# A fused linear-attention and gated-MLP kernel: projections ordered key, gate, value; first chunk products in float32; last norm tile by tile

## The chip, the cores and the metric

One core of a Trainium2 chip runs one program. The time is the device time of one execution in microseconds (us). Engines are named TensorE (PE in the profile), VectorE (DVE), ScalarE (ACT), GpSimd (POOL) and SyncE (SP, which here only issues DMAs).

## The reference

The input x is 8 sequences of 2048 tokens of 512 channels, in float32. Two layers follow each other:

```python
rkv = x @ W_rkv + b_rkv;  r, k, v = split(rkv);  r = sigmoid(r);  k = exp(k)
nu = exp(nu_log);  lam = exp(-nu);  gamma = exp(nu_log + gamma_log) - 1
u1[t] = lam * u1[t-1] + k[t] * v[t];   u2[t] = lam * u2[t-1] + k[t]
a = (u1 + gamma * k * v) / (u2 + gamma * k + 1e-6) * r
z = layernorm(x + a @ W_o + b_o)
xr, xk = mix of z[t] and z[t-1] by mu_r and mu_k
out = layernorm(z + sigmoid(xr @ W_r.T) * (relu(xk @ W_k.T)**2 @ W_v.T))
```

## The kernel before, in words

The 16384 tokens are 32 blocks of 512, 4 blocks to a sequence. The 512 channels are 4 chunks of 128 partitions. A block goes through two stages that are interleaved over two steps: in step s the three projections, the scans and the quotient of block s run, and between them the output product, the norm, the transposes and the second layer of block s-1. There are three program parts: `first_block`, `step` (written out for blocks 1 and 2, then in a loop over the sequences), and `finale`, which does the last block and all that is left. Each engine has its own order of calls, written out by hand, and waits on semaphores; nothing reorders it.

Products keep float32 accuracy by halves: every operand is split into a high part (float32r, a copy made by ScalarE) and a low part (value minus high, a subtraction by GpSimd or VectorE, written over the value). A product is then three matmuls: high by high, high by low, low by high. `project` (L1068) makes one projection of one chunk: 4 input chunks by 3 matmuls, 12 matmuls into one of four PSUM banks (bankA), used in turn; it waits until the bank's last user has read it. Of a chunk the order is key, value, gate. `rows_product` (L1097) does the same for the other four weights into bankB.

Per chunk VectorE runs `denominator` (L858: the scan of the key, the product of key and value, the denominator written into the key's buffer, the scaling by 1 + exp(-gate) and the reciprocal) and `numerator` (L884: the other scan and the sum). ScalarE runs `exp_key` (L595) and `exp_gate` (L604, two passes), GpSimd `att` (L410: numerator times reciprocal), ScalarE the high part `att_high` (L614), GpSimd the low part `att_low` (L415). `x_high` and `x_low` split the next block's input, which GpSimd does for block 1 (L408) and VectorE for the others; block 1's projections wait for them input chunk by input chunk.

At the start SyncE issues all loads, 12 of them before the rest of the projection weights. `write_columns` (L1091) is four dummy matmuls on the first weight that initialise bankB. The weights' low parts are made in block 0 and step 1 (`weight_A_low` for the projections, `weight_low` for the others). In the finale the last norm is made for two tiles of 128 tokens at a time (`inverse_std`, L419), with the last tile by itself (`last_factor`, `last_rows`).

## Time and profile before

| | us |
|---|---|
| median of 3 runs (2532.93 to 2536.94) | 2534.48 |
| the profiled execution | 2535.74 |
| its span, first to last instruction | 2533.9 |
| TensorE busy | 2510.5 (99%) |
| VectorE, ScalarE, POOL busy | 2013.6, 1267.5, 1245.6 |

The span is what the trace shows; the time of an execution has 1.84 us more around it. TensorE's busy time counts a matmul until its result is out, so that two that follow each other overlap: how far apart they start says what one costs.

### The profile page before, as it was taken

Reading aid. Unit: us, or ns where it says so; the run is one execution under the profiler, and the core shown is the slowest. Engines: PE = TensorE matmul, PEld = TensorE weight load, DVE = VectorE, ACT = ScalarE, POOL = GpSimd, SP = SyncE. Lnnn points to the kernel's source line nnn. Section 1 sums busy time; section 2 is a strip of 40 time slices with the busy share of each in tenths; the row PEclk is TensorE's granted clock in tenths of the full one; section 3 lists DMA queues with packets and bytes.
Section 4 is the critical chain, followed back from the end, with each engine's and each line's share of the span. In section 5 each row is a group of like instructions: output and inputs, shape, how many; then the busy total and the mean of one; then the engine's idle time right before and its main releaser. Section 6 shows DMA issues by size and latency. Waiting matters only on the chain.

```text
span 2533.9 us, 32904 instructions
## 1 busy us (share of the span) xinstructions
PE 2510.5 (99%) x11268; PEld 2076.7 (82%) x11268; DVE 2013.6 (79%) x2693; ACT 1267.5 (50%) x2157; POOL 1245.6 (49%) x1128
## 2 busy tenths in 40 slices
PE   7999999999999999999999999999999999999998
PEld 6888888888888888888888888888888888888877
DVE  7877888778787787887788777878777888787885
ACT  4545455444554444554545544455444555454545
POOL 6654454445454544535445444444444453545545
PEclk8999999999999999999999999999999999999999
DMA  4001110111100111111111011111111111110100
GB/s 170 26 34 51 45 39 34 34 51 50 34 34 34 51 51 34 46 38 35 51 39 45 34 35 50 50 34 34 35 50 50 34 43 34 43 51 34 51 25 34
DMA packets 57784, 110.63 MB, mean 44 GB/s; under 512 B 7040, under 2 KB 7040, under 8 KB 57088
## 3 DMA queue, kind: packets, MB, share of 16 engines
q1 hardware_dynamic: 57600, 108.31, 12.6%
q8 instruction: 100, 1.64, 0.3%
q14 instruction: 84, 0.69, 0.1%
HBM read 74.73 MB, written 33.55 MB: 43 GB/s over the span
## 4 chain that ended last, share of the span: by engine, by line
PE 98%; ACT 1%; POOL 0%; DVE 0%; DMA 0%; issue 0%; POOLq 0%; SPq 0%; DVEq 0%; ACTq 0%
PE bankA L1086 14%; PE bankA L1088 14%; PE bankA L1087 14%; PE bankB L1102 14%; PE bankB L1104 13%; PE bankB L1103 13%; PE bankB L1147 4%; PE bankB L1148 4%; PE bankB L1146 4%; PE bankB L1124 2%; PE bankA L1102 0%; PE bankA L1104 0%; PE bankA L1103 0%; POOL x_lo L408 0%; DMA wrkv_f<-in_w_rkv 0%; PE bankA L1148 0%
## 5 line engine op out<-in xcount | busy, mean ns | idle before, releaser
L1086 PE MATMUL bankA<-x_hi,wrkv_hi 128*128 128x512 f32 x1488 | 583.9, 392 | 4.7 <-POOL x_lo L408 4.7
L1088 PE MATMUL bankA<-x_hi,wrkv_lo 128*128 128x512 f32 x1488 | 580.5, 390 | 0.0
L1087 PE MATMUL bankA<-x_lo,wrkv_hi 128*128 128x512 f32 x1488 | 580.4, 390 | 0.0
L882 DVE RECIPROCAL gate<-gate 128x512 f32<-128x512 f32 x128 | 429.2, 3353 | 4.4
L413 POOL TENSOR_TENSOR att_f<-att_f,gate 128x512 f32<-128x512 f32 x128 | 209.4, 1636 | 280.1 <-DVE att_f L895 280.1
L1086 PEld LDWEIGHTS bankA<-x_hi,wrkv_hi 128*128 128x128 f32 x1488 | 280.3, 188 | 63.8 <-POOL x_lo L408 5.8
L1088 PEld LDWEIGHTS bankA<-x_hi,wrkv_lo 128*128 128x128 f32 x1488 | 280.1, 188 | 58.7
L1087 PEld LDWEIGHTS bankA<-x_lo,wrkv_hi 128*128 128x128 f32 x1488 | 280.4, 188 | 57.2
L424 POOL TENSOR_TENSOR ve<-mv,eps_ln 128x2 f32<-128x2 f32 x128 | 66.4, 519 | 462.6 <-DVE mv L907 459.6
L440 POOL TENSOR_TENSOR xk_lo<-xk_f,xk_hi 128x512 fp32r<-128x512 f32 x124 | 169.4, 1397 | 244.9 <-ACT xk_hi L667 244.9
L445 POOL TENSOR_TENSOR xr_lo<-xr_f,xr_hi 128x1024 fp32r<-128x1024 f32 x63 | 176.4, 2800 | 202.7 <-ACT xr_hi L672 202.7
L659 ACT ACTIVATE z<-z,shift,rstd 128x512 f32<-128x512 f32 x124 | 94.5, 809 | 297.6 <-POOL shift L433 297.6
L935 DVE SCALAR_TENSOR_TENSOR xr_f<-zT,vecs,xr_f 128x256 f32<-128x256 f32 x252 | 143.3, 628 | 123.7 <-ACT xr_f L644 123.7
L601 ACT ACTIVATE key<-bankA,b_sb 128x512 f32<-128x512 f32 x128 | 87.8, 686 | 283.9 <-PE bankA L1088 283.9
L879 DVE SCALAR_TENSOR_TENSOR gate<-key,gate 128x512 f32<-128x512 f32 x128 | 119.7, 935 | 125.4 <-ACT gate L612 123.2
L417 POOL TENSOR_TENSOR att_lo<-att_f,att_hi 128x512 fp32r<-128x512 f32 x128 | 186.8, 1460 | 32.8 <-ACT att_hi L616 32.8
L1102 PE MATMUL bankB<-wr_hi,xr_hi 128*128 128x512 f32 x504 | 199.5, 396 | 1.1 <-POOL xr_lo L445 1.1
L1103 PE MATMUL bankB<-wr_lo,xr_hi 128*128 128x512 f32 x504 | 196.4, 390 | 0.0
L1104 PE MATMUL bankB<-wr_hi,xr_lo 128*128 128x512 f32 x504 | 196.3, 389 | 0.0
L1102 PE MATMUL bankB<-wo_hi,att_hi 128*128 128x512 f32 x496 | 192.9, 389 | 0.0
L1103 PE MATMUL bankB<-wo_lo,att_hi 128*128 128x512 f32 x496 | 192.9, 389 | 0.0
L1104 PE MATMUL bankB<-wo_hi,att_lo 128*128 128x512 f32 x496 | 192.9, 389 | 0.0
(150 smaller groups left out, 5588.5 us busy)
## 6 DMA issues: line engine op xcount, KB each, us to landing
y<-in_x SPq DMA_DIRECT2D x128, 256.0 KB, 2.7
x_f<-in_xT SPq DMA_DIRECT2D x124, 256.0 KB, 4.0
out<-z SPq DMA_DIRECT2D x124, 256.0 KB, 2.1
wrkv_f<-in_w_rkv SPq DMA_DIRECT2D x3, 768.0 KB, 7.7
xk_f<-in_xT SPq DMA_DIRECT2D x4, 256.0 KB, 4.5
wo_f<-in_w_o SPq DMA_DIRECT2D x1, 1024.0 KB, 11.2
wk_f<-in_w_k SPq DMA_DIRECT2D x1, 1024.0 KB, 13.1
wr_f<-in_w_r SPq DMA_DIRECT2D x1, 1024.0 KB, 15.2
```

The lines of the kernel that those rows point to most:

```text
L413: pool.tensor_tensor(att_f[:, c], att_f[:, c], gate[:, c % 2], ALU.mult).then_inc(att_made, 1)
L417: pool.tensor_tensor(att_lo[:, c], att_f[:, c], att_hi[:, c], ALU.subtract).then_inc(att_lo_made, 1)
L440: pool.tensor_tensor(lo[:, c], value[:, c], hi[:, c], ALU.subtract).then_inc(xk_lo_made, 1)
L445: pool.tensor_tensor(lo[:], value[:], hi[:], ALU.subtract).then_inc(xr_lo_made, 1)
L882: dve.reciprocal(gate[:, c % 2], gate[:, c % 2]).then_inc(rec_made, 1)
L935: dve.scalar_tensor_tensor(out=value[:, c], in0=zT[:, c, HALF * half + 1:HALF * half + HALF + 1], scalar=vecs[:, 2, c:c + 1], in1=value[:, ...
L1086: pe.matmul(bank[:], w_hi, hi[:, h], start=(h == 0), stop=False)
L1087: pe.matmul(bank[:], w_hi, lo[:, h], start=False, stop=False)
L1088: last = pe.matmul(bank[:], w_lo, hi[:, h], start=False, stop=(h == NC - 1))
L1102: pe.matmul(bank[:], hi, w_hi[:, c], start=(c == 0 and not begun), stop=False, skip_group_check=begun)
L1103: pe.matmul(bank[:], hi, w_lo[:, c], start=False, stop=False, skip_group_check=begun)
L1104: last = pe.matmul(bank[:], lo, w_hi[:, c], start=False, stop=(c == NC - 1), skip_group_check=begun)
```

## The change

- The order within a chunk becomes key, gate, value (`ORDER`), with the weights' loads, high and low parts in that order too. `product` is a function of its own, called after `denominator` (in block 0 ahead of it for chunks 2 and 3). The denominator is written into the scan's buffer `u2` instead of the key's, so the key stays until the product has read it.
- In block 0 the projections of the last chunk (`EXACT`) are single float32 matmuls on the values, and so is the last chunk of block 0's output product. The low parts of these weights are made later, in step 1; block 0's input low part has a place of its own (`x_first_low`, in z's memory).
- The first weight and the five small vectors are issued by ScalarE's queue. SyncE's loads come in another order.
- `write_columns` is seven matmuls on a tile of zeros, which VectorE writes first.
- The last block's second norm is made tile by tile (`tile_gated`, `tile_statistics`, `tile_factors`, `tile_normalise`); the last tile's variance plus epsilon moves from GpSimd to VectorE. In the finale all engines have a changed order, in which also some work of the block before the last moves.

The core of the diff (indentation taken back; left out: names of semaphores, the same exchange of value and gate in bank waits, ScalarE's and VectorE's order in the finale, and `tile_gated`, `tile_statistics` and `tile_normalise`, which are the old functions for one tile):

```diff
+EXACT = (3,)
+WARM = 7
+KEY, VALUE, GATE = range(3)
+ORDER = (KEY, GATE, VALUE)
...
-return (xk_hi, xk_lo, xk_f) if s.first() else (x_hi, x_lo, x_f)
+return (xk_hi, x_first_low, xk_f) if s.first() else (x_hi, x_lo, x_f)
...
 def load_first(s):
     _, _, value = inputs(s)
     sp.dma_start(value[:, 0], xT[0, :, 0]).then_inc(x_first[0], 16)
-    load(w_A[0], wA_loaded[0])
     for c in range(1, NC):
         sp.dma_start(value[:, c], xT[0, :, c]).then_inc(x_first[c], 16)
     load(w_A[1], wA_loaded[1])
     load(w_A[2], wA_loaded[2])
-    sp.dma_start(b_sb[:], b_rkv).then_inc(s_small, 16)
-    for i, v in enumerate((nu_log, gamma_log, mu_r, mu_k)):
-        sp.dma_start(vecs[:, i], v).then_inc(s_small, 16)
     for i in range(3, len(w_A)):
         load(w_A[i], wA_loaded[i])
...
 def first_block(s):
     load_first(s)
+    load_weight(W_WO)
     load_xT(s.back(-1))
-    load_weight(W_WO)
+    load_weight(W_R)
+    load_weight(W_V)
     load_weight(W_K)
     load_rows(s, 0)
-    load_weight(W_R)
-    load_weight(W_V)
...
+def weight_A_low(c, place):
+    which = ORDER[place]
+    pool.wait_ge(wA_hi_made[place if c == 0 else 2 + c], 1)
+    if c in EXACT:
+        pool.wait_ge((k_ready, v_ready, r_ready)[which], c + 1)
     pool.tensor_tensor(wrkv_lo[:, c, which], wrkv_f[:, c, which], wrkv_hi[:, c, which], ALU.subtract)\
         .then_inc(wA_lo_made[c], 1)
...
+if i == W_WO and c == NC - 1:
+    pool.wait_ge(ready["WO"], NT)
 pool.tensor_tensor(lo[:, c], value[:, c], hi[:, c], ALU.subtract).then_inc(w_lo_made[i], 1)
...
+def tile_factors(s, tile):
+    one = slice(tile, tile + 1)
+    pool.wait_ge(ln_mean[1], s.count(NT, tile + 1))
+    pool.wait_ge(out_made, s.back(1).count(NT, tile + 1))
+    pool.tensor_tensor(ve[:, 1, one], mv[:, 1, one, 1], eps_ln[:, 0:1], ALU.add).then_inc(ln_var[1], 1)
+    pool.tensor_tensor(shift[:, 1, one], zero[:, 0:1, 0], mv[:, 1, one, 0], ALU.subtract)\
+        .then_inc(ln_negated[1], 1)
+    pool.wait_ge(ln_var[1], s.count(NH, tile + 1))
+    pool.tensor_tensor(rstd[:, 1, one], ve[:, 1, one], half_pow[:, 0:1], ALU.pow).then_inc(ln_rstd[1], 1)
+    pool.wait_ge(ln_negated[1], s.count(NH, tile + 1))
+    pool.wait_ge(ln_rstd[1], s.count(NH, tile + 1))
+    pool.tensor_tensor(shift[:, 1, one], shift[:, 1, one], rstd[:, 1, one], ALU.mult).then_inc(ln_shift[1], 1)
 def last_factor(s):
     tile = NT - 1
-    pool.wait_ge(last_mean, 1)
-    pool.tensor_tensor(ve[:, 1, tile:NT], mv[:, 1, tile:NT, 1], eps_ln[:, 0:1], ALU.add).then_inc(last_var, 1)
+    pool.wait_ge(out_made, s.back(1).count(NT, NT))
     pool.wait_ge(last_var, 1)
     pool.tensor_tensor(rstd[:, 1, tile:NT], ve[:, 1, tile:NT], half_pow[:, 0:1], ALU.pow)\
...
 def first_block(s):
     weight_A_low(1, 0)
     weight_A_low(1, 1)
-    weight_A_low(1, 2)
     weight_A_low(2, 0)
     weight_A_low(2, 1)
-    weight_A_low(2, 2)
+    weight_A_low(1, 2)
     att(s, 0)
     att_low(s, 0)
+    weight_A_low(2, 2)
     x_low(s.back(-1), 0)
-    weight_A_low(3, 0)
-    weight_A_low(3, 1)
+    x_low(s.back(-1), 1)
     att(s, 1)
+    x_low(s.back(-1), 2)
+    att_low(s, 1)
     weight_low(W_WO, 0)
-    x_low(s.back(-1), 1)
-    weight_A_low(3, 2)
+    att(s, 2)
+    x_low(s.back(-1), 3)
+    att_low(s, 2)
     weight_low(W_WO, 1)
-    att(s, 2)
-    att_low(s, 1)
-    x_low(s.back(-1), 2)
-    x_low(s.back(-1), 3)
+    att(s, 3)
     weight_low(W_WO, 2)
-    att(s, 3)
-    weight_low(W_WO, 3)
-    att_low(s, 2)
-    att_low(s, 3)
...
 if s1.first():
+    weight_low(W_R, 0)
     weight_low(W_K, 0)
+    weight_low(W_R, 1)
+    weight_A_low(3, 0)
+    weight_A_low(3, 1)
     weight_low(W_V, 0)
-    weight_low(W_R, 0)
-    weight_low(W_R, 1)
-    weight_low(W_R, 2)
-    weight_low(W_R, 3)
+    weight_low(W_V, 1)
     weight_low(W_K, 1)
+    weight_low(W_K, 2)
+    weight_low(W_K, 3)
 if s2.exists():
     residual(s2, 1)
     inverse_std(s2, 1, 1)
 inverse_std(s1, 0, 0)
 inverse_std(s1, 0, 1)
 if s1.first():
-    weight_low(W_K, 2)
-    weight_low(W_K, 3)
+    weight_low(W_R, 2)
+    weight_low(W_R, 3)
+    weight_low(W_V, 2)
+    weight_A_low(3, 2)
 att(s, 0)
-if s1.first():
-    weight_low(W_V, 1)
-    weight_low(W_V, 2)
...
+if s1.first():
+    weight_low(W_WO, 3)
...
 inverse_std(s1, 0, 1)
 att(s, 0)
 att_low(s, 0)
+mixed_keys_low(s1)
 att(s, 1)
-mixed_keys_low(s1)
+att(s, 2)
+mixed_gate_low(s1, 0)
 att_low(s, 1)
-att(s, 2)
 att_low(s, 2)
-mixed_gate_low(s1, 0)
 att(s, 3)
 att_low(s, 3)
...
+def load_constants():
+    _, _, value, source = w_A[0]
+    act.dma_start(value, source).then_inc(wA_loaded[0], 16)
+    act.dma_start(b_sb[:], b_rkv).then_inc(s_small, 16)
+    for i, v in enumerate((nu_log, gamma_log, mu_r, mu_k)):
+        act.dma_start(vecs[:, i], v).then_inc(s_small, 16)
...
-wait(act, scale_made, s.count(NC, c - 1))
+wait(act, den_made, s.count(NC, c - 1))
+wait(act, kv_made, s.count(NC, c - 1))
...
 def first_block(s):
+    load_constants()
+    weight_A_high(0)
     x_high(s, 0)
-    weight_A_high(0)
     x_high(s, 1)
     x_high(s, 2)
     x_high(s, 3)
     weight_A_high(1)
+    weight_A_high(2)
     decay()
     exp_key(s, 0)
     gamma_exp()
-    weight_A_high(2)
     weight_A_high(3)
     exp_gate(s, 0)
     weight_A_high(4)
     exp_key(s, 1)
     exp_gate(s, 1)
-    weight_A_high(5)
-    att_high(s, 0)
     x_high(s.back(-1), 0)
     x_high(s.back(-1), 1)
+    att_high(s, 0)
+    weight_high(W_WO)
+    weight_A_high(5)
     exp_key(s, 2)
+    att_high(s, 1)
     exp_gate(s, 2)
+    x_high(s.back(-1), 2)
+    weight_high(W_V)
+    weight_high(W_R)
     exp_key(s, 3)
-    weight_high(W_WO)
+    att_high(s, 2)
+    exp_gate(s, 3)
+    x_high(s.back(-1), 3)
+    att_high(s, 3)
     weight_high(W_K)
-    exp_gate(s, 3)
-    x_high(s.back(-1), 2)
-    x_high(s.back(-1), 3)
-    att_high(s, 1)
...
+    wait(dve, scale_made, s.count(NC, c))
     dve.tensor_tensor_scan(u2[:], lam_c, key[:, c % 2], state(s, 1, c), ALU.mult, ALU.add)\
         .then_inc(u2_scanned, 1)
-    dve.wait_ge(v_ready, s.count(NC, c + 1))
-    wait(dve, num_made, s.count(NC, c))
-    dve.scalar_tensor_tensor(out=kv[:], in0=bankA[(3 * c + 1) % NBANK][:], scalar=b_sb[:, 1, c:c + 1],
-                             in1=key[:, c % 2], op0=ALU.add, op1=ALU.mult).then_inc(kv_made, 1)
     dve.wait_ge(u2_scanned, s.count(NC, c + 1))
     dve.tensor_copy(carry[:, 1, c:c + 1], u2[:, TB - 1:TB]).then_inc(u2_saved, 1)
-    dve.wait_ge(kv_made, s.count(NC, c + 1))
-    dve.scalar_tensor_tensor(out=key[:, c % 2], in0=key[:, c % 2], scalar=gamma[:, c:c + 1], in1=u2[:],
+    dve.wait_ge(u2_saved, s.count(NC, c + 1))
+    dve.scalar_tensor_tensor(out=u2[:], in0=key[:, c % 2], scalar=gamma[:, c:c + 1], in1=u2[:],
                              op0=ALU.mult, op1=ALU.add).then_inc(den_made, 1)
     dve.wait_ge(den_made, s.count(NC, c + 1))
     dve.wait_ge(gate_plus1, s.count(NC, c + 1))
-    dve.scalar_tensor_tensor(out=gate[:, c % 2], in0=key[:, c % 2], scalar=EPS_DEN, in1=gate[:, c % 2],
+    dve.scalar_tensor_tensor(out=gate[:, c % 2], in0=u2[:], scalar=EPS_DEN, in1=gate[:, c % 2],
                              op0=ALU.add, op1=ALU.mult).then_inc(scale_made, 1)
     dve.wait_ge(scale_made, s.count(NC, c + 1))
     dve.reciprocal(gate[:, c % 2], gate[:, c % 2]).then_inc(rec_made, 1)
+def product(s, c):
+    dve.wait_ge(v_ready, s.count(NC, c + 1))
+    dve.wait_ge(key_exp, s.count(NC, c + 1))
+    wait(dve, num_made, s.count(NC, c))
+    dve.scalar_tensor_tensor(out=kv[:], in0=bankA[(3 * c + 2) % NBANK][:], scalar=b_sb[:, 1, c:c + 1],
+                             in1=key[:, c % 2], op0=ALU.add, op1=ALU.mult).then_inc(kv_made, 1)
...
 dve.wait_ge(last_mean, 1)
+dve.tensor_scalar(ve[:, 1, tile:NT], mv[:, 1, tile:NT, 1], EPS_LN, None, ALU.add).then_inc(last_var, 1)
...
 def first_block(s):
+    zero_operand()
     weight_A_low(0, 0)
     x_low(s, 0)
     x_low(s, 1)
     x_low(s, 2)
     x_low(s, 3)
     weight_A_low(0, 1)
+    weight_A_low(0, 2)
     constants()
-    weight_A_low(0, 2)
     gamma_minus1()
     denominator(s, 0)
+    product(s, 0)
     numerator(s, 0)
     denominator(s, 1)
+    product(s, 1)
     numerator(s, 1)
+    product(s, 2)
     denominator(s, 2)
     numerator(s, 2)
+    product(s, 3)
     denominator(s, 3)
     numerator(s, 3)
...
+tile_gated(s, 0)
+tile_gated(s, 1)
+tile_statistics(s, 0)
+tile_gated(s, 2)
+tile_statistics(s, 1)
+tile_statistics(s, 2)
 last_rows(s)
...
+if s.first() and c in EXACT:
+    pe.wait_ge(wA_loaded[place if c == 0 else 2 + c], 16)
+elif s.first() or s.second() and c in EXACT:
...
+if s.first() and c in EXACT:
+    last = pe.matmul(bank[:], w_f, value[:, h], start=(h == 0), stop=(h == NC - 1))
+else:
+    pe.matmul(bank[:], w_hi, hi[:, h], start=(h == 0), stop=False)
+    pe.matmul(bank[:], w_hi, lo[:, h], start=False, stop=False)
+    last = pe.matmul(bank[:], w_lo, hi[:, h], start=False, stop=(h == NC - 1))
...
 def write_columns():
-    pe.wait_ge(wA_hi_made[0], 1)
-    for bank in bankB:
-        pe.matmul(bank[:], wrkv_hi[:, 0, 0, 0], wrkv_hi[:, 0, 0], start=True, stop=True)\
+    pe.wait_ge(zeroed, 1)
+    for i in range(WARM):
+        pe.matmul(bankB[i % NBANK][:], x_hi[:, 0, 0:P], x_hi[:, 0], start=True, stop=True)\
             .then_inc(columns_written, 1)
...
+if name == "WO" and s.first() and c == NC - 1:
+    pe.wait_ge(att_made, NC)
+    last = pe.matmul(bank[:], att_f[:, c, tokens_at:tokens_at + P], wo_f[:, c], start=False, stop=True,
+                     skip_group_check=begun)
+    break
...
 pe.wait_ge(sum_begun, s.count(NT, tile + 1))
-if tile == 0:
-    pe.wait_ge(att_lo_made, s.count(NC, NC))
 if s.first():
+    pe.wait_ge(att_first_lo, NC - 1)
+    pe.wait_ge(w_lo_made[W_WO], NC - 1)
+elif tile == 0:
+    pe.wait_ge(att_lo_made, s.count(NC, 0))
+if s.second():
     pe.wait_ge(w_lo_made[W_WO], NC)
```

In the finale ScalarE's order changes so that `att_high(s, 3)` comes ahead of `key_square(s1, 2)` instead of behind it, and `normalise_result(s1, 0)` ahead of `tanh(s, 0)`. In a middle step VectorE calls `product(s, c)` right behind `denominator(s, c)`; there are no other changes of order in it.

## Rows read from the trace of the kernel before

**Rows 1.** The page: the span, and the chain that ended last, by engine.
```profile
span 2533.9 us, 32904 instructions
...
PE 98%; ACT 1%; POOL 0%; DVE 0%; DMA 0%; issue 0%; POOLq 0%; SPq 0%; DVEq 0%; ACTq 0%
```

**Rows 2.** TensorE's waits from 0 to 130 us: total, times, longest us.
```profile
PE bankA L1086 <- POOL x_lo L408: 4.7, 2, 4.1
PE bankA L1086 <- POOL wrkv_lo L397: 4.0, 1, 4.0
```

**Rows 3.** TensorE's waits from 2380 us to the end.
```profile
PE bankB L1102 <- POOL xr_lo L445: 1.1, 1, 1.1
PE bankA L1102 <- POOL att_lo L417: 0.8, 1, 0.8
```

**Rows 4.** The chain, its longest pieces: start, us, what.
```profile
57.13 0.80 PE bankA L1086
88.05 1.75 PE bankB L1124 x16
...
2353.13 1.75 PE bankB L1124 x16
```

**Rows 5.** Stretches: us; busy PE, PEld, DVE, ACT, POOL; granted clock; DMA share, GB/s.
```profile
43.90:49.20 5.30, 5.30 (x13) 4.14 (x14) 5.23 (x7) 0.00 (x0) 4.14 (x2) 0.50 0.00 0
54.90:62.80 7.90, 7.32 (x16) 5.29 (x17) 7.02 (x7) 2.33 (x2) 7.90 (x5) 0.50 0.19 53
80.00:2440.00 2360.00, 2359.94 (x10643) 1954.61 (x10642) 1895.59 (x2542) 1184.26 (x2031) 1142.89 (x1032) 1.00 0.12 41
```

**Rows 6.** TensorE's timeline at the start: start, us, line, operation.
```profile
6.04 2.07 PE L1094 MATMUL bankB<-wrkv_hi 128*128 128x512 f32 x4 [6.04 <-ACT wrkv_hi L575]
7.91 0.63 PE L1086 MATMUL bankA<-xk_hi,wrkv_hi 128*128 128x512 f32 x1
...
11.75 0.43 PE L1086 MATMUL bankA<-xk_hi,wrkv_hi 128*128 128x512 f32 x1
```

**Rows 7.** ScalarE and SyncE's queue at the start.
```profile
0.74 1.28 ACT L570 ACT_TABLE_LOAD   x1 [0.74 <-PEq L1266]
...
1.19 0.43 SPq L307 DMA_DIRECT2D wrkv_f<-in_w_rkv  x1
...
5.36 0.63 ACT L575 ACTIVATE wrkv_hi<-wrkv_f 128x512 fp32r<-128x512 f32 x1 [0.21 <-DMA wrkv_f<-in_w_rkv]
```

**Rows 8.** VectorE in block 0: two scans and a scaling.
```profile
26.70 1.22 DVE L864 TENSOR_TENSOR_SCAN u<-lam,key 128x512 f32<-128x512 f32 x1
...
36.60 1.21 DVE L864 TENSOR_TENSOR_SCAN u<-lam,key 128x512 f32<-128x512 f32 x1
...
39.49 0.69 DVE L879 SCALAR_TENSOR_TENSOR gate<-key,gate 128x512 f32<-128x512 f32 x1
```

**Rows 9.** POOL and ScalarE late in block 0.
```profile
46.53 2.14 POOL L413 TENSOR_TENSOR att_f<-att_f,gate 128x512 f32<-128x512 f32 x1 [0.62 <-DVE att_f L895]
...
49.39 0.69 ACT L609 ACTIVATE gate<-bankA,neg_br 128x512 f32<-128x512 f32 x1 [7.92 <-PE bankA L1088]
...
50.65 1.13 ACT L570 ACTIVATE x_hi<-x_f 128x512 fp32r<-128x512 f32 x2
...
53.60 3.47 POOL L408 TENSOR_TENSOR x_lo<-x_f,x_hi 128x512 fp32r<-128x512 f32 x2
```

**Rows 10.** POOL in the last stage.
```profile
2460.85 1.68 POOL L413 TENSOR_TENSOR att_f<-att_f,gate 128x512 f32<-128x512 f32 x1 [2.14 <-DVE att_f L895]
2463.93 1.27 POOL L417 TENSOR_TENSOR att_lo<-att_f,att_hi 128x512 fp32r<-128x512 f32 x1 [1.39 <-ACT att_hi L616]
```

**Rows 11.** POOL's first instruction for the last tile.
```profile
2529.91 0.19 POOL L450 TENSOR_TENSOR ve<-mv,eps_ln 128x1 f32<-128x1 f32 x1
```

**Rows 12.** POOL and TensorE in a middle block.
```profile
1187.04 5.46 POOL L440 TENSOR_TENSOR xk_lo<-xk_f,xk_hi 128x512 fp32r<-128x512 f32 x4 [8.13 <-ACT xk_hi L667]
...
1191.22 0.39 PE L1146 MATMUL bankB<-xk_hi,wk_hi 128*128 128x512 f32 x1
```

More of the change, by code:

```diff
@@ L57, in first, with second @@
         return self.batch is None and self.s == 0
+    def second(self):
+        return self.batch is None and self.s == 1
     def last(self):
@@ L329, in store @@
                 for tile in range(HT * half, HT * half + HT):
-                    if tile in usual(s, half):
+                    if not s.last() or tile < NT - 1:
                         sp.wait_ge(out_made, s.count(NT, tile + 1))
@@ L898, in statistics @@
             def statistics(s, which, half, rows, made):
-                tiles = usual(s, half) if which else range(HT * half, HT * half + HT)
+                tiles = range(HT * half, HT * half + HT)
                 for tile in tiles:
```

179 lines of the change are left out of this document (101 added, 78 removed).

## Prediction

> **What bounds the kernel now.** I read first the page and the chain of waits, then TensorE's own waits stretch by stretch, then each engine's timeline in the first 80 us, in one middle block and in the last 80 us. The span is 2533.9 us and the chain runs 98% over TensorE [rows 1]. Between 80 and 2440 us TensorE is busy 2359.94 of 2360 us [rows 5]; its waits all lie at the two ends: 4.0 us and twice (4.7 us together, the longest 4.1) in the first 130 us [rows 2], and 1.1 and 0.8 us in the last stage [rows 3]. A middle block takes (2353.13 - 88.05) / 29 = 78.11 us; less 1.75 us of transposes it is 336 matmuls of 0.227 us [rows 4], so a group of 12 takes 2.73 us. A change that leaves the matmuls of a middle block alone can only win at the ends. There the prize is TensorE's late start, at 7.91 us with its first projection [rows 6], its pauses, and the half clock after them: the granted clock is 0.50 from 43.9 to 49.2 us and from 54.9 to 62.8 us, after pauses of 4.0 and 4.1 us [rows 2, 5]. A matmul at that level takes (11.75 - 7.91) / 9 = 0.427 us [rows 6], 0.200 more than at the full one.
>
> The point that fixes all the rest is 57.13 us [rows 4]: there the last quarter of block 1's input low part is done, TensorE has 9 matmuls of block 1 behind it, and from there it runs on without a pause to the last stage.
>
> **The start, after the change.** ScalarE issues the first weight load and five vectors itself: six issues of about 0.43 us, the price of the same issue on SyncE's queue, from 0.74 to 3.3 us, then its table load of 1.28, so 4.6 us [rows 7]. The weight lands 4.2 us after its issue if the times now (issued 1.19, its copy started 5.36, [rows 7]) hold, at 4.9. ScalarE's copy 0.63 [rows 7], VectorE's two subtractions of about 0.6 each: the first projection starts at 6.9 instead of 7.91. The four dummy matmuls that held TensorE until then become seven on a zeroed tile; they need no load, and seven of 0.427 end near 4.3, before the data, so they cost nothing. If the table load were placed ahead of the issues, the weight would land 1.3 us later and the gain would be gone. What they do to the clock is a rival below. In the forecast the clock rises as before, 5.7 us after TensorE starts in earnest (6.04 to 11.75, [rows 6]), at 12.6. By then 13.4 matmuls are done; group 2, now the gate's, ends at 12.6 + 10.6 x 0.227 = 15.0, and the third chunk's value, group 9, at 15.0 + 7 x 2.73 = 34.1.
>
> **The first block's chain.** VectorE's chain, not TensorE, decides when block 1 can start. One chunk cycles in 36.60 - 26.70 = 9.9 us; from its scan to its scaling 39.49 - 36.60 = 2.9, from the scaling to the end of the numerator the other 7.0 [rows 8]. With the gate second, chunk 0's scaling can start at 15.1 + 1.3 (gate's two passes, 50.65 - 49.39, [rows 9]) = 16.4. Then 7.0 and the product, a pass like the scaling, 0.7 [rows 8], now behind the reciprocal: next scan at 24.1, against 26.70 now. Chunk 1 ends at 34.0. Chunk 2's product waits until 34.3, 0.3 us. POOL's att takes 2.1 [rows 9] to 36.1, ScalarE's copy 0.6 to 36.7, and only behind this copy comes gate 2, to 38.0; scale, reciprocal and numerator 7.0, to 45.0. Then in ScalarE's and POOL's new order: att 2.1 (47.1), its copy 0.6 (47.7), gate 3 1.3 (49.0), the last input copy 0.6 (49.6), and POOL's subtraction, 1.27 to 1.74 ([rows 10]; 3.47 / 2, [rows 9]): **51.2 us, against 57.13: 5.9 earlier.** The order before had both last subtractions behind a gate that waited for TensorE until 49.39 [rows 9].
>
> **Float32 products.** Twelve matmuls replace 36 in block 0's last chunk and 4 replace 12 in its output product. No row shows one of 512 columns. Below it is bounded by the float32 transposes, 1.75 / 16 = 0.109 per 128 columns, 0.44 per 512 [rows 4]; above, the three products that it replaces take 0.68, and a full product of both operands' halves has a fourth, 0.91. I take 0.91, the row of a matmul of this shape being nearer than a transpose. The Trainium skill ("FP8 and Floating Point Precision") counts "True FP32: 4 passes through PE array"; by that too it is 0.91, and by the transposes' row 0.44. In the projections 12 x 0.91 = 10.9 instead of 8.2 lies under the chain above: TensorE ends block 0 at 34.1 + 10.9 = 45.0, does 9 matmuls of block 1 by 47.0 and waits until 51.2. The cover gone, it would be +2.7. In the output product nothing covers it: 4 x 0.23 = **+0.9** (from -1.0 to +0.9). That pause is 4.2 us, like the two that dropped the clock, so the half clock after it is paid again as before: no term.
>
> **Behind it.** From 51.2, TensorE has 39 matmuls, near 11.5 us with the half clock, before the output product at 62.7. That needs att 3 and three parts of the output weight: POOL has them at about 60 (numerator 3 ends 7.0 after gate 3, at 56.0; att 2.1, one subtraction of 1.7, [rows 9]), 2.7 ahead. Then POOL has ten weight subtractions, 13 to 17 us, before the norm's factors, so to 77 at the latest. The transposes are due at 62.7 + 11.8 + 8.2 = 82.7, and the 5.7 us between hold eight short POOL instructions and four ScalarE passes, half of them side by side, some 4 us by like passes [rows 9, 11]. Slack 1.7. Loads come in another order, but the one that ScalarE reads first, the output weight, is moved ahead.
>
> **Middle blocks.** The matmuls are the same. The product moves behind the reciprocal, which delays the key mix by 0.5 to 0.7 us in VectorE's queue; behind it wait ScalarE's high and POOL's low parts and TensorE's keys. The last low part is made at 1187.04 + 5.46 = 1192.50, and needed at 1191.22 + 9 x 0.227 = 1193.26 [rows 12]: 0.76 of slack, above both. Bank waits change names (value for gate): a bank is asked for three groups later, 8.2 us, and the product is at most 7.0 behind [rows 8]. The denominator in the scan's buffer needs a wait between two VectorE instructions, under 0.1 us and hidden by the same slack. Zero.
>
> **Last stage.** POOL's new order puts the gate's low part ahead of one att_low (1.3 us or more, [rows 10]), so its 1.1 us wait goes [rows 3]; the next wait then ends on chunk 3's att_low, whose att is done at 2462.5 and its low part at 2465.2 [rows 10]. With its copy one key square earlier this is 0.7 sooner: **-0.7** for both waits together. Per-tile norm: the last tile's own chain stays; only one POOL instruction (from 2529.91, [rows 11]) goes to VectorE: **-0.1**, 0 to -0.3.
>
> **Sum.** -5.9 + 0.9 - 0.7 - 0.1 = -5.8. The profiled execution took 2535.74, 1.84 around its span, and gives 2529.9; it lies 1.26 above the median of three, 2534.48, on which basis I forecast **2528.7**.
>
> **The rivals.**
> - *The dummies release the clock.* TensorE works from about 1.3 to 4.3, pauses 2.6 us, and is at full clock for the first projection. For: pauses of 1.1 us and less kept it [rows 3]. Against: 3 us of work is less than any stretch after which a row shows it rise, 5.7, 5.3 and 7.9 us [rows 5, 6]. It would save up to 11 matmuls of 0.2, and the whole chain moves with them: -2.2, so 2526.5. The Trainium skill ("TensorE: Matmul & The Clock Gate", Part 1) says that "activity releases the throttle"; that alone does not tell these two apart, and the rows decide the chance: 0.2.
> - *The clock survives the pause in block 1.* A float32 matmul of 1.1 us or a chain that is 1.5 us faster makes the pause some 2.5 us, and the half clock goes: -2.7 (13 x 0.2), so 2526. Rows show only that 4 us lose it. 0.08.
> - *The chain is later.* POOL's subtractions at 1.74 each and slow numerators beside them put block 1's input at 53 to 54, or the table load comes first: gain 2 to 4.5, so 2530 to 2532.5. 0.22.
> - *Slower: the key mix is late in each middle block.* If the shift is over 0.76, TensorE waits in all 30 blocks; at 0.95 the waits, 30 x 0.19, cancel the gain, and at 1.2 they are 30 x 0.44 = 13 us, which ends near 2542. Against: ScalarE is busy with its previous-keys pass in that time, so the mix is not what it waits for. 0.07.
> - *The ends cancel*, as a new wait of 3 to 6 us for the output weight or the norm: 2532 to 2537. 0.05.
>
> **The numbers.** Forecast 0.38, from 2527 to 2530.5. A measurement of this kernel tells about 0.2%, 5.1 us, from no change. Faster than 2529.4: most of the forecast case, its half below 2528.7 surely, and both clock rivals: 0.57. Same: the rest of it, the late chain and the cancelled ends: 0.36. Slower: 0.07. The range runs from both clock rivals together, 2523.8, to the late end of the third, 2533.5.
>
> **What would show it.** 11239 matmuls; TensorE busy without a break from 80 to 2430 us and blocks of 78.1; float32 matmuls near 0.9; the first projection at 6.9; block 1's last input part at 51.2 with the clock at 0.50 behind it; output product without a wait near 62.7; one wait of about 1.6 in the last stage. A middle block over 78.2, or a first input part later than 53, makes the prediction wrong.

## The result, and the profile after

The changed kernel takes **2543.34 us** (median of 7 runs, 2542.72 to 2545.03) against 2534.48 (7 runs, 2532.93 to 2536.94): a ratio of 1.0035, 95% interval [1.0026, 1.0044]. It is slower, by 8.9 us; the forecast was 2528.7, in a range from 2523.8 to 2533.5. The profiled execution took 2542.95 with a span of 2541.2, 7.3 more than before [rows 1].

The page of the changed kernel: span; the chain by engine; the queue that brings instructions (packets, MB, share of 16 engines).
```profile
span 2541.2 us, 32904 instructions
...
PE 94%; issue 2%; POOL 2%; DVE 1%; ACT 0%; DMA 0%; POOLq 0%; DVEq 0%
...
q8 instruction: 106, 1.74, 0.3%
```
Against [rows 1], "issue" is new with 2% of the chain: time in which an engine waited for nothing that the profile shows. Only part of the 2% are the pauses that follow: a_pad6 below, which has none of them, still has 1% of "issue" in its chain. TensorE's waits (us in total, times, longest) answer to [rows 2, 3]. The first four rows are of 0 to 130 us, the fifth of 130 to 2380 us, where the kernel before had none at all, the last two of the last stage.
```profile
PE bankA L1172 <- POOL x_lo L417: 3.5, 1, 3.5
PE bankA L1172 <- DVE x_first_low L886: 3.1, 1, 3.1
PE bankB L1180 <- DVE x_hi L890: 1.5, 1, 1.5
PE bankB L1240 <- POOL xk_lo L449: 0.6, 2, 0.3
...
PE bankA L1173 <- issue: 14.5, 6, 2.8
...
PE bankB L1240 <- POOL xk_lo L449: 1.2, 1, 1.2
PE bankB L1193 <- ACT xk_f L740: 0.7, 1, 0.7
```
The fifth row is the result in one line: six times in the steady state TensorE stands up to 2.8 us at the second matmul of a block, though nothing is late. Six is the number of times that its loop over batches jumps back. The chain shows the same in its transposes, one group a block (start, us, what).
```profile
160.54 1.75 PE bankB L1218 x16
...
472.28 1.75 PE bankB L1218 x16
553.39 1.75 PE bankB L1218 x16
...
787.21 1.75 PE bankB L1218 x16
869.24 1.75 PE bankB L1218 x16
...
2360.40 1.75 PE bankB L1218 x16
```
The block from 472.28 to 553.39 takes 81.11 us and that from 787.21 to 869.24, four blocks later, 82.03. A block in which the loop doesn't jump takes 77.9. So the time can be split at two rows: the transposes of the second block that pass, and those 28 blocks later.

| us of the span | before | after |
|---|---|---|
| to the second block's transposes | 166.16 | 160.54 |
| 28 blocks from there | 2186.97 | 2199.86 |
| the rest | 180.77 | 180.80 |

The start gained 5.6, the end nothing, and the middle, which the prediction put at zero, lost 12.9. The next question was what the loop's jump costs in one kernel and not in the other.

TensorE's timeline of the changed kernel at the first of the six places (start, us, line, operation, idle before it):
```profile
519.91 0.39 PE L1195 MATMUL bankB<-wv_hi,xk_lo 128*128 128x512 f32 x1
520.17 0.49 PE L1172 MATMUL bankA<-x_hi,wrkv_hi 128*128 128x512 f32 x1
523.48 0.39 PE L1173 MATMUL bankA<-x_lo,wrkv_hi 128*128 128x512 f32 x1 [2.82 <-issue]
```
The block's first matmul runs and its second, which needs nothing new, comes 3.31 us later. The packets of the instruction queue carry 1.64 MB / 100 = 16.4 KB each (1.74 / 106 after). The Trainium skill ("Runtime: NRT & Kernel Launch", "Instruction fetch mechanics") tells of refills "in **16 KiB blocks** (256 instructions)" and of a fetch that a taken branch must wait for; the packets agree with the size.
### The profile page after: what moved, and what is told of

Its sections match the earlier page's. It is cut to its first block, busy times and chain, and to the rows that moved or that the text cites. A ratio compares the mean times of both kernels' runs of the same rounds, so it can differ in the third digit from the quotient of the medians.

```text
span 2541.2 us, 32904 instructions
## 1 busy us (share of the span) xinstructions
PE 2509.6 (99%) x11255; PEld 2075.1 (82%) x11255; DVE 2099.5 (83%) x2693; ACT 1270.9 (50%) x2157; POOL 1252.2 (49%) x1130
## 3 DMA queue, kind: packets, MB, share of 16 engines
q8 instruction: 106, 1.74, 0.3%
## 4 chain that ended last, share of the span: by engine, by line
PE 94%; issue 2%; POOL 2%; DVE 1%; ACT 0%; DMA 0%; POOLq 0%; DVEq 0%
PE bankB L1193 13%; PE bankB L1194 13%; PE bankB L1195 13%; PE bankA L1173 13%; PE bankA L1172 13%; PE bankA L1174 13%; PE bankB L1240 4%; PE bankB L1242 4%; PE bankB L1241 4%; PE bankB L1218 2%; POOL xk_lo L449 0%; DVE att_f L939 0%; POOL wk_lo L412 0%; DMA wrkv_f<-in_w_rkv 0%; POOL att_f L422 0%
## 5 line engine op out<-in xcount | busy, mean ns | idle before, releaser
L1173 PE MATMUL bankA<-x_lo,wrkv_hi 128*128 128x512 f32 x1488 | 580.3, 390 | 14.5 <-issue 14.5
L449 POOL TENSOR_TENSOR xk_lo<-xk_f,xk_hi 128x512 fp32r<-128x512 f32 x124 | 178.8, 1477 | 241.2 <-ACT xk_hi L707 241.2
L920 DVE SCALAR_TENSOR_TENSOR gate<-u,gate 128x512 f32<-128x512 f32 x128 | 182.9, 1429 | 104.2 <-ACT gate L647 101.8
L984 DVE SCALAR_TENSOR_TENSOR xr_f<-zT,vecs,xr_f 128x256 f32<-128x256 f32 x252 | 150.0, 655 | 113.3 <-ACT xr_f L679 113.3
L478 POOL TENSOR_TENSOR z<-t,z 128x512 f32<-128x512 f32 x124 | 169.0, 1383 | 103.2 <-DVE t L1029 103.2
L426 POOL TENSOR_TENSOR att_lo<-att_f,att_hi 128x512 fp32r<-128x512 f32 x127 | 199.1, 1568 | 35.4 <-ACT att_hi L651 35.4
L1240 PE MATMUL bankB<-xk_hi,wk_hi 128*128 128x512 f32 x496 | 193.4, 390 | 1.9 <-POOL xk_lo L449 1.7
L1242 PE MATMUL bankB<-xk_hi,wk_lo 128*128 128x512 f32 x496 | 193.0, 389 | 0.0
## 6 DMA issues: line engine op xcount, KB each, us to landing
wo_f<-in_w_o SPq DMA_DIRECT2D x1, 1024.0 KB, 12.4
```

The costliest lines, as they stand in the source:

```text
L426: pool.tensor_tensor(att_lo[:, c], att_f[:, c], att_hi[:, c], ALU.subtract)\
L920: dve.scalar_tensor_tensor(out=gate[:, c % 2], in0=u2[:], scalar=EPS_DEN, in1=gate[:, c % 2], op0=ALU.add, op1=ALU.mult).then_inc(scale_ma ...
L1173: pe.matmul(bank[:], w_hi, lo[:, h], start=False, stop=False)
L1240: pe.matmul(bank[:], wk_hi[:, c, cols], hi[:, c], start=(c == 0), stop=False)
L1242: last = pe.matmul(bank[:], wk_lo[:, c, cols], hi[:, c], start=False, stop=(c == NC - 1))
```

## The experiments

All padding is of waits on a semaphore that has long reached its value; 12 of them make 6 more instructions on the page, 474 make 237. "Left" is the number of instructions from the loop's head to the end of its piece of 256.

**a_pad6 and a_warm4: the loop's head of the changed kernel moved.** By six instructions later (place 1 of the next piece, 255 left) and six earlier (place 245, 11 left):
```
 def write_columns():
     pe.wait_ge(zeroed, 1)
+    for _ in range(12):
+        pe.wait_ge(zeroed, 1)
```
```
-WARM = 7
+WARM = 4
```

> The changed kernel with twelve waits on an already reached semaphore behind the first one of TensorE, which come to six more instructions ahead of its loop; nothing else. Theory J (the place of the loop's head in TensorE's instruction stream, which the change moved by 19 instructions, makes every jump back wait for a second instruction fetch): the six pauses of 2.0 to 2.8 us marked issue behind the jumps vanish, the time is 2543.3 less about 16 us, so 2526 to 2529, and the instruction packets of q8 fall from 106 to about 100. Rival W (a wait that the new order of work brings once in a sequence of four blocks): nothing moves, 2542 to 2545.

> The changed kernel with four dummy matmuls instead of seven, which takes six instructions away ahead of the loop. Theory J: by my count 11 instead of 5 instructions are then left in the fetched piece behind the jump, six more that TensorE can do before it waits, so each pause is shorter by 3 x 0.227 = 0.7 us and the six by 4.1: 2539, near. Rival W: 2543. Theory C (the seven dummies shorten the half clock at the start): it would be up to 2 us longer than the changed kernel from the start alone, seen in the first 20 us and not at the jumps.

**b_pad237 and b_pad243: the same with the kernel before.** 237 more instructions, laid into the projections of blocks 1 and 2, bring its head to 251 of 256; 243 bring it to place 1:
```
+spare = [474]          # 486 in b_pad243
 def project(s, c, which):
     ...
+        if s.batch is None and 1 <= s.s <= 2:
+            for _ in range(min(6, spare[0])):
+                pe.wait_ge(columns_written, NBANK)
+                spare[0] -= 1
```

> The kernel before with 474 waits on an already reached semaphore among the projections of blocks 1 and 2, which come to 237 more instructions of TensorE ahead of its loop and put the loop's head where I count it in the changed kernel, 5 instructions before the end of a piece of 256. Theory J: the kernel before gets the same six pauses of 2 to 3 us, and its time goes from 2534.5 to about 2551; q8 has about 106 packets. Rival W: it has none of the new order, so no pause, 2534.5 plus what 237 waits cost themselves.

> The same with six more instructions, 243, which put the loop's head behind the end of the piece. Theory J: no pauses, 2534.5 plus what the waits themselves cost (near nothing, since TensorE's sequencer runs ahead), and 16 us less than with 237. Rival W, or waits that cost by their number: the same as with 237 or slightly more.

**b_n30 and b_n20: how many instructions must be left.** The same edit with 424 and 444 waits.

> The kernel before with 424 satisfied waits (212 more instructions in TensorE's stream) ahead of its loop, so that 30 of the 256 instructions of the fetched piece are left from the loop's head on. The runs of the changed kernel give, with 5 left, a largest gap of matmul starts after a jump of 2.4 to 3.3 us, and, with 11 left, pauses that sum to 8.9 us over six jumps. Theory of the fetch: after a jump the next piece comes about 3.2 us after the first, and each instruction that is left buys the length of one (312.5 us for the loop's 2800 or so, 0.11 us each), so 30 hide all of it: no pause after the jumps, 2534.5 us (2532.5 to 2536.5), as with 242 left. Rival, that any second fetch close behind the jump costs its full 2.8 us: 2551 us, six pauses.

> As before, with 444 satisfied waits (222 more instructions): 20 left. Theory of the fetch: 3.2 less 20 times 0.11, about 1.0 us after each of six jumps, so about 6 us: 2540.5 us (2536 to 2544), and the largest gap after a jump near 1 us. Rival with the full price: 2551 us; if the price ends earlier than that sum says, 2534.5 us and no pause.

Measured, with the sum of TensorE's waits for "issue" between 130 and 2380 us, and the 28 blocks from the second block's transposes on:

| kernel | left | time, us | ratio to before | issue, us | 28 blocks, us |
|---|---|---|---|---|---|
| before | 242 | 2534.48 | | 0 | 2186.97 |
| b_pad243 | 255 | 2534.51 | 0.9998 [0.9989, 1.0007] | 0 | 2186.83 |
| b_n30 | 30 | 2538.34 | 1.0014 [1.0005, 1.0023] | 0.2 | 2189.41 |
| b_n20 | 20 | 2542.63 | 1.0032 [1.0020, 1.0044] | 7.4 | 2195.52 |
| b_pad237 | 5 | 2559.89 | 1.0099 [1.0083, 1.0114] | 16.8 | 2212.61 |
| a_pad6 | 255 | **2524.66** | 0.9958 [0.9945, 0.9972] | 0 | 2182.60 |
| a_warm4 | 11 | 2537.36 | 1.0008 [0.9999, 1.0017] | 8.9 | 2193.18 |
| after | 5 | 2543.34 | 1.0035 [1.0026, 1.0044] | 14.5 | 2199.86 |

The place of the loop's head decides, in both kernels and in both directions. Twelve waits that do nothing take 18.7 us off the changed kernel, and six instructions fewer of padding cost the kernel before 25 us. The three dummies that a_warm4 lacks change nothing at the start: its second block's transposes come at 160.45 us, in the changed kernel at 160.54. This doesn't hang on the fitted 95: six instructions more end the pauses in both kernels, so the head lay within the last six places of its piece. The loop has 2883 records in every version, so its end moves with its head, and no run moved one alone; but the pauses end where the head crosses into the next piece, and grow as fewer instructions are left behind it. The fetches agree: behind the first jump the third piece is asked for 4.7 us after the second in the changed kernel (536.36 after 531.70), and 23.4 us after it in a_pad6 (554.94 after 531.52).

That more instructions cost time by themselves is out: the 243 of b_pad243 cost nothing. The full price for every second fetch is out too: with 20 left the pause is 1.4 us at the longest, with 30 one of 0.2 us is left. My sum of 0.11 us for each instruction left was a little high: from 5 to 20 the longest pause of the kernel before falls from 2.8 to 1.4 us, 0.09 an instruction, so b_n20 came at 2542.6 where 2540.5 was expected, still in its bounds; b_n30's 2538.3 is above its bounds by 1.8. Its trace has 2.6 us more in the 28 blocks than b_pad243's (0.43 a jump), with six waits of TensorE's weight loads for "issue", 2.8 us together; but the profiled execution was its fastest, 2535.74, and what the median has above that stands in no trace. In the changed kernel 11 left already bring the pause down from 2.8 to 1.6, a steeper fall, and what sets the difference stays open.

b_pad237 lost more than its pauses: 2212.61 - 2186.83 = 25.8 us against 16.8. Its granted clock shows five stretches of 3.4 us at half behind five of the six pauses; 5 x 1.7 = 8.5 makes up the rest. The changed kernel has one such stretch in the loop: 14.5 + 1.7 = 16.2 of its 2199.86 - 2182.60 = 17.3 us.

**a_order: the projections of a chunk back in the order key, value, gate.** The changed kernel with the padding of a_pad6, and the product back between scan and denominator.
```
-ORDER = (KEY, GATE, VALUE)
+ORDER = (KEY, VALUE, GATE)
 ...
 def denominator(s, c):
     ...
+    product(s, c)
     dve.wait_ge(u2_scanned, s.count(NC, c + 1))
```
Bank indices and bank waits follow the order, and the separate calls of product go.

> The changed kernel with its loop's head moved out of the bad place (12 waits on a satisfied semaphore ahead, as in the run that took 2524.7 us), and the projections of a chunk back in the order key, value, gate, with the product of value and key back between the scan of the denominator and its end. Theory, by the rows of the two traces: what the middle of the kernel gained (a period of 77.94 in place of 78.10 us, some 28 times, with TensorE's wait for the low part of the mixed receptance input) came from the order, so the period goes back to 78.1 and the time up by about 4 us; ahead of block 1 the values wait a chunk longer for nothing, up to 3 us more: 2530 us (2527.5 to 2532.5). Rival, the gain of the middle came from something else (the denominator in the scan's buffer, which took a wait away): the period stays at 77.94 and the time within 1.5 us of 2524.7 apart from the first block's part.

It took 2538.11 us (2537.17 to 2539.16), ratio 1.0011 [1.0002, 1.0020], 13.4 more than a_pad6 and 5.6 above the upper bound that was expected. The rows of its chain that answer to those of a_pad6:
```profile
163.93 1.75 PE bankB L1209 x16
...
2352.86 1.75 PE bankB L1209 x16
```
```profile
160.66 1.75 PE bankB L1220 x16
...
2343.26 1.75 PE bankB L1220 x16
```
The 28 blocks take 2188.93 us in a_order and 2182.60 in a_pad6: 78.18 and 77.95 a block; before, 78.11. The start is 3.3 later and the end, 182.74 in place of 180.74, 2.0, which was not expected at all. So the gain of the middle did come from the order, of the projections and of the product's place together (no run parts the two), and it was worth 6.3, not 4. What it took away shows in the waits of TensorE's weight loads between 130 and 2380 us (us in total, times, longest), first the kernel before, then a_order, then a_pad6:
```profile
PEld bankB L1102 <- POOL xr_lo L445: 5.2, 20, 0.3
PEld bankB L1102 <- issue: 2.2, 8, 0.3
```
```profile
PEld bankB L1184 <- POOL xr_lo L454: 6.6, 20, 0.3
PEld bankB L1184 <- issue: 2.7, 8, 0.4
```
```profile
PEld bankA L1172 <- issue: 0.4, 2, 0.2
```
Twenty times in 28 blocks a weight load of the gate's product came up to 0.3 us late, behind the low part of its input. With the gate computed second that wait is gone, and with it some 9 us of late loads, of which 6.3 were time. A reading of the queues suggests why (ScalarE makes this input's high part behind the gates' exponentials, which now come sooner), but no run took that apart. For the prediction I had read only the matmuls' rows of the waits and "busy 2359.94 of 2360" [rows 5]; a late weight load makes no pause there and shows in the loads' own rows alone.

**a_keys: in the last stage, the low part of the mixed keys ahead of attention's.**
```
     att(s, 0)
+    mixed_keys_low(s1)
     att_low(s, 0)
-    mixed_keys_low(s1)
     att(s, 1)
```

> The changed kernel with its loop's head moved (as in the run of 2524.7 us), and in the last stage GpSimd makes the low part of the mixed keys of the last block but one ahead of the low part of attention's first chunk of the last block. Theory: the order that the change gave there makes TensorE wait 1.2 us for this low part, which goes; the wait for its float part on ScalarE (0.7 us) stays: about 1.2 us less from the last loop's end to the end, 2523.5 us. Rival: attention's low part is then late and takes the wait over, nothing changes or up to 1 us more: 2524.7 to 2525.7 us. The stage in the trace decides, since the total can't tell 1 us surely.

2529.11 us (2527.6 to 2530.36), ratio 0.9974 [0.9965, 0.9983]: 4.5 more than a_pad6. The theory fell. TensorE's waits in the last stage of a_keys:
```profile
PE bankA L1195 <- POOL att_lo L426: 4.1, 1, 4.1
PE bankB L1195 <- ACT xk_f L740: 0.7, 1, 0.7
```
The 1.2 us wait is gone, and one of 4.1 for attention's last low part stands behind it, with 3.4 us of half clock after it. From the last loop's transposes (2341.45 in its timeline) to the end it takes 184.9 us, in a_pad6 (2343.09) 180.9. The rival had the mechanism right and the price, up to 1 us, far too low. So in the last stage two low parts wait for the same engine, and to put one first is paid by the other.

**a_xhigh: the last part of block 1's input first on ScalarE.**
```
     exp_key(s, 3)
+    x_high(s.back(-1), 3)
     att_high(s, 2)
     exp_gate(s, 3)
-    x_high(s.back(-1), 3)
```

> The changed kernel with its loop's head moved (as in the run of 2524.7 us), and ScalarE makes the high part of block 1's last input chunk right behind the last exponential of the key of block 0, ahead of attention's high part 2 and the last gate. In the trace of the changed kernel this chunk's low part ends at 50.84 us and TensorE stands 3.5 us, then runs at the lower clock for some 2.8 us. Theory: the chunk is ready about 2.5 us earlier, the pause falls to about 1 us, and the half clock behind it goes too, since it comes of the pause: about 4 us less, 2520.7 us. Rival: the pause shrinks by 2.5 us and the clock falls all the same, or the later attention parts (high part 2, the last gate) hold block 0's output product up by as much: 2522.2 us, or 2524.7 us with a new wait of TensorE for attention's last low part.

2525.79 us (2524.29 to 2526.0), ratio 0.9965 [0.9951, 0.9978]; a_pad6 has 0.9958. TensorE's waits in its first 120 us, without the two for the dummies and the first projection:
```profile
PE bankB L1195 <- POOL wo_lo L412: 2.1, 1, 2.1
PE bankA L1172 <- POOL x_lo L417: 1.7, 1, 1.7
PE bankB L1242 <- POOL xk_lo L449: 1.2, 3, 0.6
PE bankB L1220 <- ACT z L688: 1.0, 1, 1.0
```
The pause fell from 3.5 to 1.7 us, and the half clock behind it is gone, as the theory had it: in this trace the granted clock stays full from there to the end of the matmuls. But 2.1, 1.0 and 1.2 us of new waits in block 1 take it all back, as the rival's second half had it, if under other names. The cause of the first stands in the two engines' timelines, GpSimd and VectorE of a_xhigh:
```profile
45.96 2.19 POOL L417 TENSOR_TENSOR x_lo<-x_f,x_hi 128x512 fp32r<-128x512 f32 x1
48.11 1.74 POOL L426 TENSOR_TENSOR att_lo<-att_f,att_hi 128x512 fp32r<-128x512 f32 x1
49.80 1.73 POOL L412 TENSOR_TENSOR wo_lo<-wo_f,wo_hi 128x512 fp32r<-128x512 f32 x1
...
47.31 1.38 DVE L916 SCALAR_TENSOR_TENSOR u<-key,gamma,u 128x512 f32<-128x512 f32 x1
48.73 1.66 DVE L920 SCALAR_TENSOR_TENSOR gate<-u,gate 128x512 f32<-128x512 f32 x1
```
GpSimd's subtractions now run beside VectorE's two passes of two inputs, and both pay: 2.19 in place of 1.40 us, and 1.38 and 1.66 in place of 0.75 and 0.69 in a_pad6. VectorE, whose last scan starts 1.0 us earlier than in a_pad6, starts the reciprocal behind it 0.6 later (50.43 against 49.85), and the third low part of the output weight ends 0.4 later (59.26 against 58.91) for a TensorE that asks for it some 4 us sooner. The Trainium skill ("SBUF — State Buffer", "SBUF: two separate sides") says that the two engines share a pair of ports, which one of them holds for a whole instruction; the longer times of these rows agree, though they don't show how long either holds it.

**a_xhigh_wo: the third low part of the output weight in GpSimd's idle time.**
```
     att_low(s, 2)
     weight_low(W_WO, 1)
+    weight_low(W_WO, 2)
     att(s, 3)
-    weight_low(W_WO, 2)
```

> The changed kernel with its loop's head moved and the last input chunk's high part earlier, and GpSimd makes the third low part of the output weight ahead of attention's last chunk in block 0, not behind it. In the run without this second move the half clock was gone, but TensorE stood 2.1 us for this low part, which ended at 59.3 us, while GpSimd stood idle for 4.4 us ahead of attention's last chunk. Theory: the low part is made in that idle time, the wait goes, and the gain of the earlier input chunk comes to the end: 2523.5 us (2521.5 to 2525), and TensorE's block 1 starts some 2 us earlier. Rival: the low part then runs beside VectorE's reciprocal and scan, delays the last numerator and with it attention's last chunk; the wait changes its name only: 2525.5 us or more.

2524.73 us (2524.36 to 2525.11), ratio 0.9962 [0.9948, 0.9975]. That lies within the theory's bounds, but the gain didn't come. The wait for the weight went, but its name only changed: TensorE now waits 2.0 us for ScalarE's z, the norm's result, and behind that pause it runs at the half clock for 3.4 us, which a_xhigh did not have. The 16 transposes behind the wait take 2.71 us in place of 1.75:
```profile
79.36 2.71 PE bankB L1220 x16
```
The waits for the mixed keys in block 1 are gone in this trace. So the next chain in block 1, the norm, is as late as the one removed.

**a_sploads: the first weight and the vectors back on SyncE's queue.**
```
 sp.dma_start(value[:, 0], xT[0, :, 0]).then_inc(x_first[0], 16)
+load(w_A[0], wA_loaded[0])
```
and the vectors' loads behind the third piece of the weight; load_constants goes.

> The changed kernel with its loop's head moved (as in the run of 2524.7 us), and the first weight and the vectors back on SyncE's queue. Theory: the move saved nothing, since the weight landed 5.0 us after its issue from ScalarE in place of 4.2 us from SyncE behind the first input part; the first projection starts at 7.9 us as in both traces, and the total stays within 0.5 us of 2524.7 us. Rival, as the prediction had it: the move was worth 1.0 us and the later issue of the first input chunks costs more, the first projection starts at 8.9 us or so, 2525.7 us.

2525.08 us (2524.73 to 2525.4), ratio 0.9963 [0.9950, 0.9977]. The move is worth nothing in the total. The first projection starts at 7.56 us, in the six traces with the loads on ScalarE and the same padding at 7.77 to 8.06: if anything, SyncE's queue is the earlier. The weight is issued at 1.19 us and lands 4.25 later, at 5.44; in the changed kernel at 0.75, and lands 5.02 later, at 5.77.

**a_best: a_keys and a_xhigh together.**

> The changed kernel with its loop's head moved, the last input chunk's high part earlier, and in the last stage the mixed keys' low part ahead of attention's. Theory: the two parts lie 2,400 us apart and add: 4 and 1.2 us less than 2524.7, 2519.5 us (2517.5 to 2522), faster than both kernels (the kernel before 2535, the changed one 2543.3). Rival, if each of the two is worth nothing by itself: 2524.7 us.

2529.60 us (2528.42 to 2531.92), ratio 0.9981 [0.9972, 0.9990]: 10 above what was expected, and as a_keys alone, since a_xhigh is worth nothing. The best version stays a_pad6, 2524.66 us, with a_xhigh_wo level: 0.42% faster than the kernel before and 0.73% than the changed one.

## Why the prediction was wrong

**The step that failed.** "Middle blocks. The matmuls are the same. [...] Zero", with "TensorE busy without a break from 80 to 2430 us". I followed the data through the middle and not the instructions. Six jumps of the loop cost 17.3 us there (2199.86 - 2182.60, after against a_pad6), because the change made TensorE's stream ahead of the loop 19 instructions shorter and put the loop's head 5 instructions ahead of the end of its piece. Against this the 28 blocks gained 2186.97 - 2182.60 = 4.4 us by the new order, which was put at zero too. Neither was among the rivals, though the prediction's own sign of being wrong, a middle block over 78.2, came true in six blocks. The rival that ended slower, near 2542, has about the right time for a wrong reason: the last low part of the mixed keys did slip, but only from 0.76 to 0.4 us ahead (made at 1188.90 + 5.83 = 1194.73, needed at 1193.10 + 9 x 0.227 = 1195.14), and no middle block waits for it.

**What the other steps gave.** Without the jumps the sum of the change is -5.6 at the start, -4.4 in the middle and 0.0 at the end, -10.0, and a_pad6 measured 2524.66 - 2534.48 = -9.8. The prediction had -5.8.

- *The start*: 6.9 predicted, 7.89 measured, so nothing gained on 7.91. The term that was mis-sized is the load:
```profile
0.75 5.02 DMA wrkv_f<-in_w_rkv
5.79 0.64 ACT wrkv_hi L609
6.45 0.69 DVE wrkv_lo L880
7.14 0.61 DVE x_first_low L886
...
7.89 0.77 PE bankA L1172
```
In this part of the chain the weight takes 5.02 us from issue to landing, not 4.2. It was issued in the same moment as the first input part, 0.75 and 0.76 us, not 0.43 behind it; a_sploads, with the old place on SyncE's queue, has 4.25. Whether the queue or the moment makes the difference no run shows. ScalarE was free 0.4 us before it landed, so the table load was not the cause.

- *The first block's chain*: block 1's last input part at 51.2 predicted, 50.84 measured, from 57.13. The time is right partly by luck. The second chunk's scan starts at 25.17 (24.1 predicted), its numerator ends at 35.7 (34.0), the third chunk's scaling starts at 39.2 (38.0) and its numerator ends at 45.5 (45.0). Then GpSimd's att takes 1.30 us, not 2.1, and its last subtraction 1.40, at the low end of what was allowed for, and this made up what had been lost.
```profile
46.99 0.39 PE L1174 MATMUL bankA<-x_hi,wrkv_lo 128*128 128x512 f32 x1
50.84 0.79 PE L1172 MATMUL bankA<-x_hi,wrkv_hi 128*128 128x512 f32 x1 [3.46 <-POOL x_lo L417]
51.44 0.63 PE L1173 MATMUL bankA<-x_lo,wrkv_hi 128*128 128x512 f32 x1
...
53.57 0.57 PE L1172 MATMUL bankA<-x_hi,wrkv_hi 128*128 128x512 f32 x1
53.98 0.39 PE L1173 MATMUL bankA<-x_lo,wrkv_hi 128*128 128x512 f32 x1
```
The pause is 3.5 us (4.2 predicted), and behind it the matmuls run at 0.63 us of the half level for some 3 us, then at 0.39 again. The half clock was counted as before, where it lasted 5.7 us more behind 57.13 [rows 5]; half of the difference, 1.4 us, is gained. Then block 1 loses 1.1 by the mixed keys (below). With 57.13 - 50.84 = 6.3 that makes -6.3 - 1.4 + 0.9 + 1.1 = -5.7, and the second block's transposes came 5.6 us earlier where -5.9 + 0.9 = -5.0 was forecast. That a shorter pause would keep the clock was a rival at 0.08; a_xhigh, with 1.7 us, kept it, and it was no gain in the end.

- *Float32 products*: 0.91 us each predicted. Each leaves two records, so the trace has 11255 matmuls and not 11239. The twelve projections, and the two matmuls behind them:
```profile
34.87 10.46 PE L1170 MATMUL bankA<-xk_f,wrkv_f 128*128 128x512 f32 x24
44.76 0.79 PE L1172 MATMUL bankA<-x_hi,wrkv_hi 128*128 128x512 f32 x1
45.39 0.40 PE L1173 MATMUL bankA<-x_lo,wrkv_hi 128*128 128x512 f32 x1
```
Less the 0.227 us of the one matmul between, (45.39 - 0.23 - 34.87) / 12 = 0.86 us each. They lay under VectorE's chain, as said. In the output product one stands among nine products of halves, and two tiles start 2.95 us apart:
```profile
63.32 1.02 PE L1189 MATMUL bankB<-wo_f,att_f 128*128 128x512 f32 x2
66.27 1.02 PE L1189 MATMUL bankB<-wo_f,att_f 128*128 128x512 f32 x2
```
2.95 - 9 x 0.227 = 0.91, so the forecast's +0.9 was right to the tenth.

- *Behind it*: the output product started without a wait and no norm was late, as said. But the mixed keys' low parts were, in block 1: two waits of 0.3 us, with the matmuls between 91.9 and 94.9 us spread so that 1.2 us are lost (1.1 more than before). That chain stood in no step of the prediction. a_xhigh and a_xhigh_wo show how thin the slack is: a few us earlier and three chains are late in the one, the norm by 2.0 us in the other.

- *Last stage*: -0.8 predicted, 0.0 measured. The two waits of [rows 3], 1.1 and 0.8 us, went as forecast, and two others of 1.2 and 0.7 took their places, one for the mixed keys' low part, behind attention's in GpSimd's new order. The prediction said "one wait of about 1.6"; it looked only at the engines that had been late, not at what the new order put behind. The -0.7 is the term that was mis-sized. a_keys shows the price of the other order.

- *The dummies and the clock*: a rival at 0.2. In the profiled execution the first twelve matmuls ran at the half level, 0.43 us apart, and the clock rose near 13.0 us (12.6 predicted, 11.8 before), so it did not come true. In other executions of the same first instructions the clock is full for the first few matmuls and then falls (below); the 2.2 us come in none.

## What to carry to other kernels

When an edit changes the number of instructions ahead of a loop, ask where in the fetched pieces of 256 the loop's head lands, and compare the blocks with a jump in them with those without; a pause "issue" at a loop's jump, with nothing late, is this, and a few idle waits ahead of the loop cure it. Try that padding before judging any edit of such a kernel: here it was worth 18.7 us, more than all that the edit was meant to do, and without it a gain of 9.8 us reads as a loss of 8.9. And read the weight loads' waits beside the matmuls': a middle that is busy 100% still had 4 to 6 us in it.
